# A selective scan in which GpSimd takes three of its sixteen output products, and its preparation runs a step earlier

## The chip, the cores and the metric

The kernel runs on one core of a Trainium2 chip. Its engines are TensorE (PE: matrix products and transposes into PSUM), VectorE (DVE), ScalarE (ACT), GpSimd (POOL) and SyncE (SP), which here only starts transfers. Each engine runs its own list of instructions in order, and semaphores hold an instruction back until another engine has done what it needs. The metric is the device time of one launch in microseconds (us). Before the change it was 1448.95 us, the median of three runs (1447.45 to 1464.47).

## The reference, cut to what matters

Two transformer-like layers run on 16 sequences of 256 positions with 128 features. Layer 0 has a decaying linear attention and a mixture of experts, layer 1 a selective scan (Mamba) and a second mixture of experts. The change touches the selective scan of layer 1 alone:

```python
proj = x @ W_in.T                       # x_s (256), z (256), B (16), C (16), dt (8)
x_s = silu(conv(x_s) + conv_b)          # depthwise, 4 taps
dt = softplus(dt @ W_dt.T + b_dt)
for t in range(256):                    # 256 channels d, 16 states n
    h[d, n] = exp(dt[t, d] * A[d, n]) * h[d, n] + dt[t, d] * B[t, n] * x_s[t, d]
    y[t, d] = sum_n h[d, n] * C[t, n]
y = (y + x_s * D) * silu(z)
out = layernorm(residual + y @ W_out.T)
```

## The kernel before, in words

`scan_phase` handles the 16 sequences one after another, b = 0 to 15. The 256 channels lie as two halves (h) on the 128 partitions, time along the free axis. A sequence is walked in eight **steps**, j = 0 to 7, of two states (n) each, so an operand of a step has 2 x 2 x 256 = 1024 elements in each partition. In a step

- ACT makes the decays `dA` (`decays`, four exponentials), three steps ahead, in a ring of four buffers;
- POOL multiplies the transposed input `dtuT` by four columns of B (`inputs`, line 1409, four instructions on 256 elements), also three steps ahead, in a ring of four (`dbuT`);
- PE copies the rows of C of this step to all partitions (`C_rows`, bank bC), transposes `dbuT` of the next step (`turn_inputs`, line 1532) and adds up the products of the step before (`sum_states`, line 1550);
- DVE runs the recurrence (`recur`, line 1181, one scan over 1024 elements into `hs`) and then the product with C (`times_C`, line 1189, 1024 elements into `hc`). `hs` and `hc` have two buffers each, used by even and odd steps.

Between these stands the work of the neighbouring sequences. `prepare(step, b + 1)` makes the next sequence's inputs: step 0 (normalized input `xn`, its transpose, and at 0.5 `hT`), 1 (projection of B, C and dt: `low`, `BT`, `bc`), 2 (ACT's six instructions of softplus, from `soft` = |x| to the last `soft`), 3 (convolution, PE), 4 (silu into `u` and `z`, between two loads of ACT's tables), 5 (`dtu` transposed into `dtuT`). `finish(step, b - 1)` ends the sequence before: 0 (DVE `yz`, PE transposes, ACT `yzT`), 1 (PE output projection), 2 (DVE statistics, ACT `olnv` and `orstd`), 3 (DVE `oshift`, ACT `oh`). POOL's shares are `split` and `keep` at j = 2, `cubic` at 3, `steps` (line 1369, dt) at 4, `times_u` (line 1383, `dtu`) and `residual` (lines 1389 to 1397) at 5. DVE's `lesser` (line 1154, `least`) is in step 4.

What sets the order is only how the code is written: each engine has a function `body` that walks j and issues its parts in turn. There is no scheduler. DVE's body is `recur`, then `finish`, then `lesser` if j is 4, then `times_C`; it waits in place wherever an input is late.

## Time and profile before

| | us |
|---|---|
| median of three runs | 1448.95 |
| the profiled execution, own time | 1469.19 |
| its span, first to last instruction | 1467.0 |
| DVE busy | 893.7 (61%) |
| PE busy | 1130.1 (77%) |
| ACT busy | 687.8 (47%) |
| POOL busy | 561.8 (38%) |
| scans of the 16 sequences (line 1181), first to last start | 514.6 to 999.9 |

The span counts from the first to the last instruction of one profiled execution. That execution took 1469.19 us, 20.24 us more than the median of the runs without a profile. The shares are averages over ten stages with different limits. The selective scan is one of them, about a third of the span. Busy time of PE is modelled, and overlaps between its instructions are counted once.

### The profile page before, as it was taken

The numbers are of one execution on the slowest core, as the hardware profiler recorded it, in microseconds if no ns is written. First come the engines' busy times: TensorE is split into PE (matmuls) and PEld (weight loads), VectorE is DVE, ScalarE is ACT, GpSimd is POOL, SyncE is SP. The second block draws the span as 40 slices with busy tenths as digits, with TensorE's granted clock in tenths as the row PEclk, the third lists the DMA queues.
The fourth block names the chain that finished last, engine by engine and source line by source line (L and its number), as shares of the span: only waits on it lengthen the run. The fifth ranks groups of instructions, "written<-read, shape, count | busy, mean of one in ns | idle before, by whom it ended". The sixth has DMA issues, their size and how long they took to land. (4 is left out here: it accounts for less than half of the span.)

```text
span 1467.0 us, 23954 instructions
## 1 busy us (share of the span) xinstructions
PE 1130.1 (77%) x6776; PEld 857.3 (58%) x6777; DVE 893.7 (61%) x1786; ACT 687.8 (47%) x1527; POOL 561.8 (38%) x882
## 2 busy tenths in 40 slices
PE   2887885689978688888888888883374799999860
PEld 1555554334448578777888877773243666666640
DVE  2355553711039599999999999993376633333327
ACT  1334432233324587888778887771241033333320
POOL 1000000300012277777877778770000155555540
PEclk9667775799989789999999999996555599999995
DMA  6000000011010200000000000002310011111115
GB/s 181 0 1 1 0 1 1 0 44 43 29 29 0 58 1 1 1 0 0 0 0 0 0 0 0 0 0 90 97 33 17 6 35 39 36 39 38 38 48 181
DMA packets 41607, 39.87 MB, mean 27 GB/s; under 512 B 4041, under 2 KB 37474, under 8 KB 41202
## 3 DMA queue, kind: packets, MB, share of 16 engines
q1 hardware_dynamic: 32466, 22.37, 5.2%
q0 software_dynamic: 4608, 9.45, 2.3%
q10 hardware_dynamic: 4496, 7.60, 1.5%
q8 instruction: 18, 0.29, 0.1%
q14 instruction: 19, 0.16, 0.0%
HBM read 30.44 MB, written 8.96 MB: 27 GB/s over the span
## 5 line engine op out<-in xcount | busy, mean ns | idle before, releaser
L1181 DVE TENSOR_TENSOR_SCAN s_hs<-s_dA,bank 128x1024 f32<-128x1024 f32 x128 | 291.9, 2280 | 10.2 <-PE bank L1532 10.1
L1409 POOL TENSOR_SCALAR s_dbuT<-s_dtuT,s_BT 128x256 f32<-128x256 f32 x512 | 239.9, 492 | 11.0 <-ACT s_dtuT L1264 8.8
L1292 ACT ACTIVATE s_dA<-s_dt,aneg 128x255 f32<-128x255 f32 x512 | 213.6, 498 | 0.6 <-DVE s_hs L1181 0.4
L1982 POOL DMA_INDIRECT x_xg<-hf_rows,x_src x72 | 69.7, 968 | 236.9 <-issue 170.6
L1532 PE MATMUL bank<-const,s_dbuT 128*128 128x128 f32 x1024 | 139.7, 282 | 26.0 <-POOL s_dbuT L1409 26.0
L1189 DVE TENSOR_TENSOR s_hc<-s_hs,bank 128x1024 f32<-128x1024 f32 x128 | 156.1, 1220 | 5.2 <-PE bank L1520 0.9
L2022 PE MATMUL bank<-w,x_xT 128*128 x288 | 128.4, 569 | 19.0 <-ACT x_xT L2064 16.3
L1550 PE MATMUL bank<-const,s_hc 128*128 128x128 f32 x1024 | 138.0, 280 | 2.2 <-DVE s_hc L1189 2.2
L1532 PEld LDWEIGHTS bank<-const,s_dbuT 128*128 128x128 f32 x1024 | 119.8, 145 | 32.7 <-issue 26.3
L1550 PEld LDWEIGHTS bank<-const,s_hc 128*128 128x128 f32 x1024 | 120.7, 145 | 2.4 <-DVE s_hc L1189 2.4
L2060 ACT ACTIVATE x_a<-bank 128x448 f32<-128x448 f32 x72 | 39.1, 543 | 161.6 <-PE bank L2022 156.7
L484 POOL COPY xn<-xb 128x512 f32 (+1 forms) x8 | 4.9, 612 | 213.3 <-ACT xb L500 213.3
L2022 PEld LDWEIGHTS bank<-w,x_xT 128*128 128x128 f32 x288 | 50.1, 194 | 56.5 <-issue 56.0
L1989 POOL DMA_INDIRECT y_rows<-x_y,x_dst x72 | 71.0, 987 | 29.3 <-issue 22.4
L2044 PE MATMUL bank<-w2d,x_hT 112*128 x576 | 77.8, 278 | 2.6 <-DVE x_y L2092 2.1
L965 POOL COPY yst<-yT 128x512 f32 (+1 forms) x16 | 16.1, 1031 | 166.1 <-POOLq L103 123.2
L920 DVE COPY yT<-bank 128x512 f32 x16 | 11.1, 692 | 110.5 <-PE bank L900 110.5
L2044 PEld LDWEIGHTS bank<-w2d,x_hT 112*128 112x128 f32 x576 | 69.9, 191 | 5.5 <-issue 4.4
L2080 DVE COPY x_src<-from_row 128x1 uint32 (+1 forms) x72 | 11.1, 154 | 100.8 <-PE bank L2031 96.0
L912 ACT ACTIVATE g<-bank 128x512 f32<-128x512 f32 x64 | 38.2, 597 | 58.7 <-PE bank L893 58.7
L893 PE MATMUL bank<-xin,w 128*128 x128 | 59.2, 618 | 5.9 <-DMA w<-in_w 5.9
L1520 PE MATMUL bank<-s_bc,spread 128*128 128x256 bf16 x256 | 50.7, 281 | 16.7 <-DVE s_hc L1189 14.7
(301 smaller groups left out, 2273.6 us busy)
## 6 DMA issues: line engine op xcount, KB each, us to landing
w<-in_w SPq DMA_DIRECT2D x16, 256.0 KB, 3.1
o_yr<-y_rows SPq DMA_DIRECT2D x8, 512.0 KB, 3.9
w<-in_w ACTq DMA_DIRECT2D x1, 3584.0 KB, 13.3
x_res<-in_x SPq DMA_DIRECT2D x4, 512.0 KB
gate<-gates_d SPq DMA_DIRECT2D x2, 1024.0 KB, 5.6
s_gate<-gates_d SPq DMA_DIRECT2D x2, 1024.0 KB, 7.4
hf_rows<-r_rows SPq DMA_DIRECT2D x8, 256.0 KB, 2.2
out<-o_o ACTq DMA_DIRECT2D x8, 256.0 KB, 2.4
```

The source lines that it names most:

```text
L893: pe.matmul(ps[h][:, :], w1[:, k, h * P:(h + 1) * P], m.xin[:, 2 * r + k, a * N:(a + 1) * N], start=True, stop=True).then_inc(hidden[h], 1)
L1181: dve.tensor_tensor_scan(flat(hs[:, j % 2]), flat(dA[:, j % RING]), bDbu[j % 2], 0.0, ALU.mult, ALU.add).then_inc(S["scanned"], 1)
L1189: dve.tensor_tensor(hc[:, j % 2], hs[:, j % 2], bC[:, :].rearrange("p (n t) -> p n t", n=2).unsqueeze(1).broadcast_to([P, NH, 2, L]), ALU. ...
L1292: ins = act.activation(dA[:, j % RING, h, n, 1:], dt[:, k, h, 1:], ACT.Exp, scale=m.aneg[:, h, 2 * j + n:2 * j + n + 1])
L1409: ins = pool.tensor_scalar(dbuT[:, j % RING, c, n, :], dtuT[:, k, c, :], BT[:, k, c, 2 * j + n:2 * j + n + 1], 1.0, ALU.mult, ALU.mult)
L1520: mm = pe.matmul(bC[:, n * L:(n + 1) * L], m.spread[:, 2 * j + n, :], bc[:, k, :], start=True, stop=True)
L1532: mm = pe.transpose(out[:, h, n, c * P:(c + 1) * P], dbuT[:, j % RING, c, n, h * P:(h + 1) * P], ident)
L1550: mm = pe.matmul(part(c, h), hc[:, j % 2, h, n, c * P:(c + 1) * P], ident, is_transpose=True, start=False, stop=(j == SCAN_J - 1 and n == ...
L1982: pool.indirect_dma_start(xg[k][:], None, m.hf_rows[:, :], bass.IndirectOffsetOnAxis(ap=src[k][:, 0:1], axis=0)).then_inc(S["rows"][k], 16)
L1989: pool.indirect_dma_start(m.y_rows[:, :], bass.IndirectOffsetOnAxis(ap=dst[k][:, 0:1], axis=0), y[k][:], None).then_inc(S["sent"][k], 16)
L2022: mm = pe.matmul(ps[2 * k + i][:, 0:I1], xT[:, k, :], m.w13[:, bass.ds(e * 2 + i, 1), :].rearrange("p e i -> p (e i)"), start=True, stop=True)
L2044: mm = pe.matmul(ps[5][:, 0:D], hT[:, k, i, :], m.w2d[:, bass.ds(e * NIC + i, 1), :].rearrange("p e d -> p (e d)"), start=(i == 0), stop=( ...
```

## The change

SHARED = (0, 5, 6) names three steps. In these DVE multiplies only the first of the two states by C (512 elements instead of 1024). The second is multiplied by a new function on POOL, `shared_C(b, j)`, which stands in POOL's step j + 1 behind `inputs`. It cannot read PSUM, so it takes its C row from SBUF: SP copies three rows of `low` to DRAM and from there to all 128 partitions (`Crow`), once per sequence. PE spreads one C row instead of two in these steps, and adds the shared product up two steps later (`sum_shared`). Two more waits are new on DVE: the scan of step j + 2 waits until POOL has read the buffer of step j (`shared`), and the product of step j + 2 until PE has read it (`y_shared`).

Beside this, parts of `prepare` move. PE does the projection still at j = 0, but ahead of step 1's recurrence work and behind `finish(0)`, and dt's product at j = 1 instead of 2; half of the convolution moves to j = 4; the skip product with D moves from `sum_states(0)` to `sum_states(1)`. ACT does softplus (prepare 2) at j = 1 instead of at the end of j = 2, and at j = 4 and 5 it does silu and the copy to `dtuT` ahead of the decays instead of behind them.

```diff
@@ -1060,2 +1060,3 @@
 AHEAD = 3
+SHARED = (0, 5, 6)
 
@@ -1070,2 +1071,3 @@
 
+
     with ExitStack() as ctx:
@@ -1099,2 +1101,4 @@
         hc = sb("hc", [P, 2, NH, 2, L])
+        Crow = sb("Crow", [P, 2, len(SHARED), L])
+        C_d = nc.dram_tensor("C_rows", (2, len(SHARED), L), F32).ap()
         yz = sb("yz", [P, NCH, DI])
@@ -1106,3 +1110,4 @@
                  "u_ready z_ready dt_ps pos abs ln soft dt_ready dtu_ready dtuT_ps dtuT hi r1 mid bc_parts oln gate "
-                 "yz yzT_ps yzT out_ps ostats ost ors oshift o_read og done").split()
+                 "yz yzT_ps yzT out_ps ostats ost ors oshift o_read og done "
+                 "C_kept C_spread shared y_shared").split()
         S = {n: sem(n) for n in names}
@@ -1180,2 +1185,6 @@
                 dve.wait_ge(S["dA_ready"], 8 * b + j + 1)
+                if j == 0:
+                    dve.wait_ge(S["shared"], len(SHARED) * b + 1)
+                elif j - 2 in SHARED:
+                    dve.wait_ge(S["shared"], len(SHARED) * b + SHARED.index(j - 2) + 2)
                 dve.tensor_tensor_scan(flat(hs[:, j % 2]), flat(dA[:, j % RING]), bDbu[j % 2], 0.0,
@@ -1188,5 +1197,10 @@
                     dve.wait_ge(S["y_part"], 8 * b + j - 1)
-                dve.tensor_tensor(hc[:, j % 2], hs[:, j % 2],
-                                  bC[:, :].rearrange("p (n t) -> p n t", n=2).unsqueeze(1).broadcast_to(
-                                      [P, NH, 2, L]), ALU.mult).then_inc(S["hc_ready"], 1)
+                if j == 0 and not first:
+                    dve.wait_ge(S["y_shared"], len(SHARED) * b)
+                elif j - 2 in SHARED:
+                    dve.wait_ge(S["y_shared"], len(SHARED) * b + SHARED.index(j - 2) + 1)
+                own = 1 if j in SHARED else 2
+                dve.tensor_tensor(hc[:, j % 2, :, 0:own], hs[:, j % 2, :, 0:own],
+                                  bC[:, 0:own * L].rearrange("p (n t) -> p n t", n=own).unsqueeze(1).broadcast_to(
+                                      [P, NH, own, L]), ALU.mult).then_inc(S["hc_ready"], 1)
 
@@ -1235,2 +1249,4 @@
                     act.wait_ge(S["bc_ps"], b + 1)
+                    if not (isinstance(b, int) and b == 0):
+                        act.wait_ge(S["C_kept"], 16 * len(SHARED) * b)
                     act.activation(low[:], bX[:, 0:L], ACT.Identity, bias=ident[:, 32 + RDT:33 + RDT])\
@@ -1297,2 +1313,4 @@
                 for j in range(SCAN_J):
+                    if prepares and j in (4, 5):
+                        prepare(j, b + 1, 1 - k)
                     if j + AHEAD < SCAN_J:
@@ -1301,10 +1319,10 @@
                         decays(b + 1, 1 - k, j + AHEAD - SCAN_J, True)
-                    if prepares and j != 2:
-                        prepare(j, b + 1, 1 - k)
-                    if not first:
-                        finish(j, b - 1, 1 - k)
                     if prepares and j == 0:
+                        prepare(0, b + 1, 1 - k)
                         prepare(0.5, b + 1, 1 - k)
-                    if prepares and j == 2:
-                        prepare(j, b + 1, 1 - k)
+                    if prepares and j == 1:
+                        prepare(1, b + 1, 1 - k)
+                        prepare(2, b + 1, 1 - k)
+                    if not first:
+                        finish(j, b - 1, 1 - k)
 
@@ -1332,2 +1350,22 @@
 
+            def spread_C(b, k):
+                sp.wait_ge(S["low"], b + 1)
+                if not (isinstance(b, int) and b == 0):
+                    sp.wait_ge(S["C_spread"], 16 * len(SHARED) * b)
+                for i, j in enumerate(SHARED):
+                    row = NST + 2 * j + 1
+                    sp.dma_start(C_d[k, i:i + 1, :], low[row:row + 1, :]).then_inc(S["C_kept"], 16)
+                sp.wait_ge(S["C_kept"], 16 * len(SHARED) * (b + 1))
+                if not (isinstance(b, int) and b <= 1):
+                    sp.wait_ge(S["shared"], len(SHARED) * (b - 1) + 1)
+                for i in range(len(SHARED)):
+                    sp.dma_start(Crow[:, k, i, :], C_d[k, i, :].partition_broadcast(P)).then_inc(S["C_spread"], 16)
+
+            spread_C(0, 0)
+            spread_C(1, 1)
+            with sp.Fori(0, PAIRS - 1, 1) as r:
+                spread_C(2 * r + 2, 0)
+                spread_C(2 * r + 3, 1)
+            sp.wait_ge(S["C_spread"], 16 * len(SHARED) * B)
+
         @block.gpsimd
@@ -1412,2 +1450,15 @@
 
+            def shared_C(b, k, j, first):
+                i = SHARED.index(j)
+                pool.wait_ge(S["C_spread"], 16 * len(SHARED) * (b + 1))
+                pool.wait_ge(S["scanned"], 8 * b + j + 1)
+                if j >= 2:
+                    pool.wait_ge(S["y_part"], 8 * b + j - 1)
+                elif not first:
+                    pool.wait_ge(S["y_part"], 8 * b + j - 1)
+                    pool.wait_ge(S["y_shared"], len(SHARED) * b)
+                pool.tensor_tensor(hc[:, j % 2, :, 1], hs[:, j % 2, :, 1],
+                                   Crow[:, k, i, :].unsqueeze(1).broadcast_to([P, NH, L]), ALU.mult)\
+                    .then_inc(S["shared"], 1)
+
             def body(b, k, first, prepares):
@@ -1422,2 +1473,4 @@
                         inputs(b + 1, 1 - k, j + AHEAD - SCAN_J, True)
+                    if j - 1 in SHARED:
+                        shared_C(b, k, j - 1, first)
                     if prepares and j == 2:
@@ -1433,2 +1486,3 @@
             pool.sem_inc(S["done"], 1)
+            pool.sem_inc(S["shared"], 1)
             pool.wait_ge(S["gate"], 32)
@@ -1469,6 +1523,6 @@
                     mm.then_inc(S["dt_ps"], 1)
-                if step == 3:
+                if step in (3, 3.5):
                     pe.wait_ge(S["abs"], b + 1)
                     pe.wait_ge(S["pos"], b + 1)
-                    for h in range(NH):
+                    for h in range(NH)[:1] if step == 3 else range(NH)[1:]:
                         for tap in range(KCONV):
@@ -1476,3 +1530,4 @@
                                            hT[:, k, tap:tap + L], start=(tap == 0), stop=(tap == KCONV - 1))
-                    mm.then_inc(S["xs_ps"], 1)
+                    if step == 3.5:
+                        mm.then_inc(S["xs_ps"], 1)
                 if step == 4:
@@ -1518,3 +1573,3 @@
                     pe.wait_ge(S["hc_ready"], 8 * b + j)
-                for n in range(2):
+                for n in range(1 if j in SHARED else 2):
                     mm = pe.matmul(bC[:, n * L:(n + 1) * L], m.spread[:, 2 * j + n, :], bc[:, k, :],
@@ -1537,6 +1592,6 @@
                 part = lambda c, h: bY[:, c * DI + h * P:c * DI + (h + 1) * P]
-                if j == 0:
+                if j == 0 and not first:
+                    pe.wait_ge(S["yz"], b)
+                if j == 1:
                     pe.wait_ge(S["u_ready"], 2 * b + 2)
-                    if not first:
-                        pe.wait_ge(S["yz"], b)
                     for c in range(NCH):
@@ -1544,5 +1599,5 @@
                             pe.matmul(part(c, h), u[:, k, h, c * P:(c + 1) * P], m.dskip[:, h, :],
-                                      start=(c == 0 and h == 0), stop=False, skip_group_check=True)
+                                      start=False, stop=False, skip_group_check=True)
                 pe.wait_ge(S["hc_ready"], 8 * b + j + 1)
-                for n in range(2):
+                for n in range(1 if j in SHARED else 2):
                     for c in range(NCH):
@@ -1550,3 +1605,3 @@
                             mm = pe.matmul(part(c, h), hc[:, j % 2, h, n, c * P:(c + 1) * P], ident,
-                                           is_transpose=True, start=False,
+                                           is_transpose=True, start=(j == 0 and n == 0 and c == 0 and h == 0),
                                            stop=(j == SCAN_J - 1 and n == 1), skip_group_check=True)
@@ -1554,2 +1609,10 @@
 
+            def sum_shared(b, j):
+                pe.wait_ge(S["shared"], len(SHARED) * b + SHARED.index(j) + 2)
+                for c in range(NCH):
+                    for h in range(NH):
+                        mm = pe.matmul(bY[:, c * DI + h * P:c * DI + (h + 1) * P], hc[:, j % 2, h, 1, c * P:(c + 1) * P],
+                                       ident, is_transpose=True, start=False, stop=False, skip_group_check=True)
+                mm.then_inc(S["y_shared"], 1)
+
             def body(b, k, first, prepares):
@@ -1557,2 +1620,6 @@
                     C_rows(b, k, j, first)
+                    if j - 2 in SHARED:
+                        sum_shared(b, j - 2)
+                    elif j == 0 and not first:
+                        sum_shared(b - 1, SCAN_J - 2)
                     if j + 1 < SCAN_J:
@@ -1565,8 +1632,12 @@
                         sum_states(b - 1, 1 - k, SCAN_J - 1, False)
-                    if prepares:
-                        prepare(j, b + 1, 1 - k)
+                    if prepares and j == 0:
+                        prepare(0, b + 1, 1 - k)
                     if not first:
                         finish(j, b - 1, 1 - k, prepares)
+                    if prepares:
+                        for step in {0: (1,), 1: (2,), 3: (3,), 4: (3.5, 4), 5: (5,)}.get(j, ()):
+                            prepare(step, b + 1, 1 - k)
 
             def last(b, k):
+                sum_shared(b, SCAN_J - 2)
                 sum_states(b, k, SCAN_J - 1, False)
@@ -1575,4 +1646,4 @@
 
-            for j in range(SCAN_J):
-                prepare(j, 0, 0)
+            for step in (0, 1, 2, 3, 3.5, 4, 5):
+                prepare(step, 0, 0)
             turn_inputs(0, 0, 0, True)
```

The first place is POOL from the end of `residual` on (`x_res<-x_res,s_og`), that is its steps 5 to 7 and the first two of the next sequence. Before:

```order
L1397 TENSOR_TENSOR x_res<-x_res,s_og 128x256
L1405 REGISTER_ALU
L1409 TENSOR_SCALAR s_dbuT<-s_dtuT,s_BT 128x256 x8
L1405 REGISTER_ALU
L1409 TENSOR_SCALAR s_dbuT<-s_dtuT,s_BT 128x256 x8
L1405 REGISTER_ALU
L1409 TENSOR_SCALAR s_dbuT<-s_dtuT,s_BT 128x256 x4
```

And with the change:

```order
L1435 TENSOR_TENSOR x_res<-x_res,s_og 128x256
L1443 REGISTER_ALU
L1447 TENSOR_SCALAR s_dbuT<-s_dtuT,s_BT 128x256 x8
L1454 REGISTER_ALU
L1460 TENSOR_TENSOR s_hc<-s_hs,s_Crow 128x2x256
L1443 REGISTER_ALU
L1447 TENSOR_SCALAR s_dbuT<-s_dtuT,s_BT 128x256 x4
L1454 REGISTER_ALU
L1456 REGISTER_ALU
L1460 TENSOR_TENSOR s_hc<-s_hs,s_Crow 128x2x256
```

The product of step 5 now stands behind `residual` and behind the eight `dbuT` instructions of the next sequence's steps 0 and 1; the product of step 6 follows four more.

The second place is ACT in the steps 1 and 2, from the projection's outputs to `orstd`, the scale of the layer norm of the sequence before. Before:

```order
L1236 ACTIVATE s_low<-bank,const 128x256
L1238 ACTIVATE s_BT<-bank 128x32
L1240 ACTIVATE s_bc<-bank 128x256
L1289 REGISTER_ALU
L1292 ACTIVATE s_dA<-s_dt,aneg 128x255 x4
L1273 ISA
L1274 ACTIVATE s_olnv<-s_omv,eps 128x2
L1276 ACTIVATE s_orstd<-s_olnv 128x2
L1244 ACTIVATE s_soft<-bank 128x512
```

And with the change:

```order
L1256 ACTIVATE s_bc<-bank 128x256
L1260 ACTIVATE s_soft<-bank 128x512
L1261 ACTIVATE s_pos<-bank 128x512
L1263 ACTIVATE s_e<-s_soft 128x512
L1265 ACTIVATE s_sq<-s_e,eps 128x512
L1266 ACTIVATE s_over<-s_e,eps 128x512
L1268 ACTIVATE s_soft<-s_over,eps 128x512
L1305 REGISTER_ALU
L1308 ACTIVATE s_dA<-s_dt,aneg 128x255 x4
L1289 ISA
L1290 ACTIVATE s_olnv<-s_omv,eps 128x2
L1292 ACTIVATE s_orstd<-s_olnv 128x2
```

The six softplus instructions, which stood behind `orstd`, now stand ahead of it and of the decays of step 5.

## Rows read from the trace of the kernel before

**Rows 1.** Busy time by engine in a stretch of the scan stage.
```profile
core 0: us, PE busy (x) PEld busy (x) DVE busy (x) ACT busy (x) POOL busy (x), PEclk, DMA share, GB/s
800.00:900.00 100.00, 88.81 (x666) 79.59 (x665) 95.87 (x80) 80.46 (x179) 76.92 (x141) 0.98 0.00 0
```

**Rows 2.** Single lines: duration in ns (min/median/max), first and last start.
```profile
L1181 DVE TENSOR_TENSOR_SCAN s_hs<-s_dA,bank x128: 2278/2280/2289, 514.6 to 999.9; 128x1024 f32<-128x1024 f32 x128
...
L1189 DVE TENSOR_TENSOR s_hc<-s_hs,bank x128: 1210/1221/1223, 516.9 to 1002.2; 128x1024 f32<-128x1024 f32 x128
```

**Rows 3.** Timeline, DVE (start, us, line, operation): scans that open sequences 1 and 15.
```profile
544.21 2.28 DVE L1181 TENSOR_TENSOR_SCAN s_hs<-s_dA,bank 128x1024 f32<-128x1024 f32 x1
...
974.10 2.28 DVE L1181 TENSOR_TENSOR_SCAN s_hs<-s_dA,bank 128x1024 f32<-128x1024 f32 x1
```

**Rows 4.** Timeline, DVE: step 2 of one sequence to step 1 of the next.
```profile
829.61 2.28 DVE L1181 TENSOR_TENSOR_SCAN s_hs<-s_dA,bank 128x1024 f32<-128x1024 f32 x1
...
833.73 2.28 DVE L1181 TENSOR_TENSOR_SCAN s_hs<-s_dA,bank 128x1024 f32<-128x1024 f32 x1
835.92 0.13 DVE L1174 SCALAR_TENSOR_TENSOR s_oshift<-s_omv,s_orstd 128x2 f32<-128x2 f32 x1
...
837.18 2.28 DVE L1181 TENSOR_TENSOR_SCAN s_hs<-s_dA,bank 128x1024 f32<-128x1024 f32 x1
839.37 0.88 DVE L1154 TENSOR_TENSOR s_least<-s_small,s_soft 128x512 f32<-128x512 f32 x1
...
841.54 2.28 DVE L1181 TENSOR_TENSOR_SCAN s_hs<-s_dA,bank 128x1024 f32<-128x1024 f32 x1
...
851.90 2.28 DVE L1181 TENSOR_TENSOR_SCAN s_hs<-s_dA,bank 128x1024 f32<-128x1024 f32 x1
854.54 0.69 DVE L1160 TENSOR_TENSOR s_yz<-bank,s_z 128x512 f32<-128x512 f32 x1 [0.36 <-PE bank L1550]
856.28 2.28 DVE L1181 TENSOR_TENSOR_SCAN s_hs<-s_dA,bank 128x1024 f32<-128x1024 f32 x1
```

**Rows 5.** Timeline, POOL, the same sequence, steps 5 to 7.
```profile
844.42 1.27 POOL L1383 TENSOR_TENSOR s_dtu<-s_dt,s_u 128x512 f32<-128x512 f32 x1 [1.68 <-ACT s_u L1256]
...
848.61 10.91 POOL L1409 TENSOR_SCALAR s_dbuT<-s_dtuT,s_BT 128x256 f32<-128x256 f32 x24 [0.30 <-ACT s_dtuT L1264]
```

**Rows 6.** Timeline, ACT, the same sequence, steps 2 to 6.
```profile
832.71 0.29 ACT L1274 ACTIVATE s_olnv<-s_omv,eps 128x2 f32<-128x2 f32 x1
...
834.60 0.60 ACT L1244 ACTIVATE s_soft<-bank 128x512 f32<-128x512 f32 x1 [1.37 <-PE bank L1467]
...
838.23 1.69 ACT L1292 ACTIVATE s_dA<-s_dt,aneg 128x255 f32<-128x255 f32 x4
...
843.51 0.84 ACT L1256 ACTIVATE s_u<-bank,bcol 128x256 f32<-128x256 f32 x2
...
847.75 0.57 ACT L1264 ACTIVATE s_dtuT<-bank 128x512 f32<-128x512 f32 x1
```

**Rows 7.** Timeline, PE, step 7 and the next sequence's steps 0 to 3.
```profile
850.58 1.09 PE L1532 MATMUL bank<-const,s_dbuT 128*128 128x128 f32 x8 [1.60 <-POOL s_dbuT L1409]
...
855.29 0.66 PE L1500 MATMUL bank<-const,s_yz 128*128 128x128 f32 x4 [0.57 <-DVE s_yz L1160]
...
859.29 0.60 PE L1457 MATMUL bank<-s_hT,w_in 128*128 128x256 f32 x2
...
863.57 1.13 PE L1467 MATMUL bank<-s_low,wdt 9*128 9x256 f32 x4
...
866.60 3.62 PE L1475 MATMUL bank<-s_hT,wc 128*128 128x256 f32 x16
```

**Rows 8.** Where PE's granted clock was 0.50: busy times, and DVE's timeline beside them.
```profile
820.00:822.00 2.00, 2.00 (x11) 2.00 (x11) 1.52 (x2) 2.00 (x6) 2.00 (x6) 0.50 0.00 0
...
820.66 2.29 DVE L1181 TENSOR_TENSOR_SCAN s_hs<-s_dA,bank 128x1024 f32<-128x1024 f32 x1 [0.48 <-PE bank L1532]
...
824.42 0.69 DVE L1160 TENSOR_TENSOR s_yz<-bank,s_z 128x512 f32<-128x512 f32 x1 [1.47 <-PE bank L1550]
```

More of the change, by code:

```diff
@@ L1565, in body @@
                         sum_states(b - 1, 1 - k, SCAN_J - 1, False)
-                    if prepares:
-                        prepare(j, b + 1, 1 - k)
+                    if prepares and j == 0:
+                        prepare(0, b + 1, 1 - k)
                     if not first:
                         finish(j, b - 1, 1 - k, prepares)
+                    if prepares:
+                        for step in {0: (1,), 1: (2,), 3: (3,), 4: (3.5, 4), 5: (5,)}.get(j, ()):
+                            prepare(step, b + 1, 1 - k)
             def last(b, k):
+                sum_shared(b, SCAN_J - 2)
                 sum_states(b, k, SCAN_J - 1, False)
```

3 lines of the change are left out of this document (1 added, 2 removed).

## The prediction

> **What bounds the kernel now.** I read the busy times by stretch first. In the scan stage DVE is busy for 95.87 of 100 us, PE for 88.81, ACT for 80.46 and POOL for 76.92 [rows 1]. So DVE sets the pace here, and nothing outside this stage is touched. The first and the last start of the scans, 514.6 and 999.9 us, bound what the change can reach [rows 2]. From the opening scan of sequence 1 to that of sequence 15 there are 14 sequences in 429.89 us, 30.71 us each [rows 3].
>
> Next comes DVE's timeline through one undisturbed sequence. I write T0 to T7 for the starts of its eight scans. A plain step takes 3.45 us: T5 to the next T0 is 10.36 us for three [rows 4]. Step 2 takes 4.12 us because of the statistics, step 4 4.36 us because of `least`, step 0 4.38 us because of `yz`, of which 0.36 us is a wait for PE [rows 4]. The sum is 4.38 + 3.45 + 4.12 + 3.45 + 4.36 + 10.36 = 30.12 us. The mean is 0.6 us above it, and rows 8 show why: in some sequences PE's granted clock is 0.50 (1.2 GHz instead of 2.4 GHz) around the turn to the next sequence, and `yz` starts 3.76 us behind its scan (824.42 against 820.66) instead of 2.64 us (854.54 against 851.90) [rows 4, 8]. Ahead of it PE stood still for 1.60 us, waiting for POOL's `dbuT` [rows 7].
>
> **What the change gives.** A product with C over 1024 elements takes 1.22 us [rows 2]. The nearest row of half that size with one operand in PSUM is `yz`, 0.69 us [rows 4]. So each of the three shared steps gives DVE 0.53 us, a step of 2.92 us instead of 3.45, and a sequence 1.6 us, if nothing waits. PE spreads three C rows fewer; this I cost at nothing, since PE then only waits longer for DVE.
>
> **What it adds on POOL.** Three products of 128x512, like `dtu`'s 1.27 us [rows 5]. Both operands and the output are in SBUF there too, so I take 1.27 for each, between 0.69 (DVE's time for the size, below which POOL will not come) and 2 us. The Trainium skill advises against such a move (GPSIMD Engine Reference, section 4.1, Engine selection: elementwise work with two inputs belongs on VectorE, about twice as slow on GpSimd). Twice 0.69 would be 1.38, an estimate from that page, and would add 0.1 us to a sequence; the trace's ratio is 1.84, so it agrees.
>
> More than its length, the product's place counts. The product of step 5 stands in POOL's list behind `dtu`, the three instructions of `residual` and eight `dbuT` of the next sequence, as the first pair of order listings shows. DVE's scan of step 7 now waits for it, since it overwrites the same `hs` buffer, and behind that scan everything on DVE is queued. I follow this chain from T4.
>
> 1. PE begins its part of step 4 at T4 + 0.15 (the product of step 3 is then done). From the dt product to the convolution is 3.03 us (863.57 to 866.60), of which the dt product itself is 1.0; so C rows, transposes and sum take 2.0 [rows 7]. The half of the convolution that is now in step 4 takes half of 3.62 us [rows 7]. It is done by T4 + 4.1, and ACT begins `u` at T4 + 4.2.
> 2. From `u` to the start of the `dtuT` copy ACT needs 4.24 us (843.51 to 847.75): `u`, `z`, a table load and four decays. The new order has the same instructions between them. The copy takes 0.57 [rows 6]: done at T4 + 9.0.
> 3. POOL begins `dtu` 0.91 us after `u` (844.42 against 843.51), at T4 + 5.1, and the `dbuT` 4.19 us after that (848.61), `residual` being between [rows 5, 6]: T4 + 9.3. Moving silu up has brought this point forward: before, it was T4 + 11.43 (848.61 against 837.18) [rows 4, 5].
> 4. 24 `dbuT` take 10.91 us, 0.455 each [rows 5]. Eight take 3.64, then the product 1.27: T4 + 14.2. DVE starts scan 7 at T4 + 14.3.
>
> DVE by itself would be there at 4.36 + 2.92 + 2.92 = T4 + 10.2. **So it waits 4.1 us in each sequence.** The next T0 comes 3.45 later, T4 + 17.75; the product of step 6 (four more `dbuT` and 1.27, to T4 + 17.3) is just in time.
>
> **The second new wait.** Softplus now stands ahead of the decays of step 5 and of `orstd` on ACT (second pair of order listings), but DVE still takes `oshift` in step 3, and behind it stands the product that ends the step. From T0: `yz` starts at 2.7 (four transposes more, but PE comes earlier), and step 0 takes 2.7 + 1.74 - 0.53 = 3.9 [rows 4]. PE begins the `yzT` transposes 0.75 later, and the projection 0.42 after that, at 3.9. From the projection to the dt product is 4.28 us (859.29 to 863.57), less 0.44 for half a group of transposes: 7.7 [rows 7]. The dt product takes 1.13, so `soft` starts at 8.9 [rows 7]. From `soft` to the decays are 3.63 us (834.60 to 838.23), the decays keep ACT 1.6, `olnv` and `orstd` 0.5 [rows 6]: 14.65. DVE would start `oshift` 2.19 behind T3 [rows 4], and T3 is 3.9 + 3.45 + 4.12 = 11.5, so at 13.7. It waits 1.0 us, and T4 is at 11.5 + 3.45 + 1.05 = 16.0.
>
> **The sum.** A sequence takes 14.3 + 3.45 + 16.0 = 33.75 us at full clock. PE now idles some 3.8 us ahead of the product of step 5, where 1.60 us of idling preceded the low clock in about one sequence of three. When the clock is low there, everything from `yz` on is 1.1 us later (3.76 - 2.64) [rows 4, 8]. I take that for three sequences in four: 0.85, together 34.6. The Trainium skill (TensorE: Matmul & The Clock Gate, What's actually happening) says that the clock is held back by default and activity releases it; by this every sequence would pay, 4 us more in all.
>
> Against 30.71 this is 3.9 more in each of 14 sequences, 54.6 us. Sequence 0 has no `finish` and pays about 2 us, sequence 15 prepares nothing, so POOL is free and 1.6 us are gained; these cancel. The profiled execution would go from 1469.19 to 1524 us. The median lies 20.24 us under the profiled time, and both shift alike: 1448.95 + 55 = **1504 us**, 3.8% slower.
>
> The two copies of C between SBUF and DRAM are costed at nothing: `low` is ready in step 1, and POOL needs the rows in the next sequence's step 0, over 20 us later. If this cover failed, POOL would wait for them in front of everything of step 1.
>
> **The rivals.**
>
> - *Only the wait of step 7 is real* (0.2). ACT reaches `orstd` in time, because PE's chain from `yz` to the dt product is shorter than added up here; the margin is only 1.0 us. Then 34.6 - 1.05 = 33.55, 14 x 2.84 = 40: 1489 us; with the clock low as seldom as before, 1482.
> - *DVE stays the bound* (0.08, the other side). Point of decision: POOL ends the product of step 5 by T4 + 10.2. Then the steps are 30.12 - 1.6 = 28.5, 14 x 2.2 + 3.2 = 34 us less: 1415 us, 2.3% faster. For it speaks that silu moves up and DVE is at 96%. Against it: `dbuT` would have to start by T4 + 5.3, but `least` alone ends at T4 + 3.07 (839.37 + 0.88 against 837.18) [rows 4], and after it come `dt` and `dtu` of about 1.27 each and `residual`.
> - *The waits nearly cancel the gain* (0.14): `residual` or the copy to `dtuT` costs POOL less than in the old order, and the chain is 2 to 3 us shorter. Then the time is 1430 to 1475 us.
> - *Both waits, and PE falls behind as well* (0.1): low clock in all sequences and for longer, 1 us more each: 1518 to 1535 us.
> - *Both waits as added up* (0.48): 1490 to 1518 us.
>
> That the change doesn't do what it says is hardly possible: the order shows the three products and the halved operands.
>
> The range is 1466 to 1520 us; it leaves out the faster case, the lower part of the near-cancelling one and the upper part of the last. About 2% is what a measurement of this kernel can tell from no change; within it lie 1420 to 1478 us. Faster by over 2%: 0.06; within 2%: 0.16; slower: 0.78.
>
> **What would show it.** The line of DVE's scan has idle time of some 55 us before it, released by POOL's `hc`, all of it at step 7; with none there the forecast falls. `oshift` has some 14 us of idle before it, released by ACT's `orstd`. The halved products take 0.69 us and POOL's 1.27. From one opening scan to the next are 34 to 35 us. PE waits for the same POOL product just ahead. If the step 7 scan starts within 11 us of T4, the chain through `dtu` and `residual` was wrong.

## The result and the profile after

The changed kernel takes 1509.51 us (median of 4 runs, 1504.30 to 1512.35). The kernel before took 1450.03 us beside it (4 runs, 1447.45 to 1464.47). The ratio is 1.036, 95% interval 1.032 to 1.041: **slower**. The ratio is estimated with its interval and isn't exactly the quotient of the medians; by it the loss is 53 us, by the medians 59.5, and 55 were forecast.

The profiled execution took 1509.2 us. First the page's span and busy times:

```profile
span 1507.4 us, 24350 instructions
PE 1137.1 (75%) x6728; PEld 865.8 (57%) x6729; DVE 869.2 (58%) x1786; ACT 689.5 (46%) x1527; POOL 615.4 (41%) x930
```

The span grew by 40.4 us only, but this understates the loss: in the profile of before, the opening scan starts at 514.6 us [rows 2], here at 503.3, and the change gives no engine other work ahead of it. From the opening scan to the last one are 485.3 us before and 539.8 now (503.32 to 1043.11), **54.5 us more**. This is the number that the sum of the prediction has to meet. It lies between the two estimates of the loss; runs of the kernel before differ by 17 us among themselves, so I assign no more than this.

The groups of instructions in the scan stage (line, engine, operation, operands, count | busy us, mean ns | idle time just before them in us, and what ended it):

```profile
L1190 DVE TENSOR_TENSOR_SCAN s_hs<-s_dA,bank 128x1024 f32<-128x1024 f32 x128 | 291.8, 2280 | 75.7 <-POOL s_hc L1460 66.5 <-PE bank L1587 9.1
L1203 DVE TENSOR_TENSOR s_hc<-s_hs,bank 128x1024 f32<-128x1024 f32 x80 | 97.3, 1216 | 4.8 <-PE bank L1614 2.1 <-PE bank L1575 1.6
L1203 DVE TENSOR_TENSOR s_hc<-s_hs,bank 128x512 f32<-128x512 f32 x48 | 32.9, 684 | 1.6 <-PE bank L1575 0.5
L1460 POOL TENSOR_TENSOR s_hc<-s_hs,s_Crow 128x512 f32<-128x512 f32 x48 | 61.0, 1272 | 5.3 <-DVE s_hs L1190 3.6 <-issue 1.6
L1179 DVE SCALAR_TENSOR_TENSOR s_oshift<-s_omv,s_orstd 128x2 f32<-128x2 f32 x16 | 4.9, 306 | 11.9 <-ACT s_orstd L1292 11.9
```

The halved product takes 684 ns on DVE and the other half 1272 ns on POOL, so each of the 48 shared products saves DVE 0.53 us of work, as costed: 25 us in all. Ahead of the scans, however, DVE now stands idle for 66.5 us, waiting for POOL's `hc`, and 11.9 us ahead of `oshift`. The saving was real, and the waits were three times as large.

The waits of steady sequences, 560 to 1020 us (total us, times, longest):

```profile
DVE s_hs L1190 <- POOL s_hc L1460: 61.1, 14, 4.4
PE bank L1614 <- POOL s_hc L1460: 55.2, 14, 4.0
...
DVE s_oshift L1179 <- ACT s_orstd L1292: 10.5, 13, 0.8
```

There is one wait of 4.4 us in a sequence, and one of 0.8. The timelines of ACT, DVE, POOL and PE show where, in a sequence whose T4 is 863.79:

```profile
862.17 0.20 ACT L1292 ACTIVATE s_orstd<-s_olnv 128x2 f32<-128x2 f32 x1
862.41 0.33 DVE L1179 SCALAR_TENSOR_TENSOR s_oshift<-s_omv,s_orstd 128x2 f32<-128x2 f32 x1 [0.80 <-ACT s_orstd L1292]
863.79 2.27 DVE L1190 TENSOR_TENSOR_SCAN s_hs<-s_dA,bank 128x1024 f32<-128x1024 f32 x1
...
867.83 0.84 ACT L1272 ACTIVATE s_u<-bank,bcol 128x256 f32<-128x256 f32 x2 [1.87 <-PE bank L1529]
868.75 1.28 POOL L1421 TENSOR_TENSOR s_dtu<-s_dt,s_u 128x512 f32<-128x512 f32 x1 [0.74 <-ACT s_u L1272]
...
872.22 0.57 ACT L1280 ACTIVATE s_dtuT<-bank 128x512 f32<-128x512 f32 x1
873.07 3.65 POOL L1447 TENSOR_SCALAR s_dbuT<-s_dtuT,s_BT 128x256 f32<-128x256 f32 x8 [0.44 <-ACT s_dtuT L1280]
876.68 1.27 POOL L1460 TENSOR_TENSOR s_hc<-s_hs,s_Crow 128x512 f32<-128x512 f32 x1
877.98 2.29 DVE L1190 TENSOR_TENSOR_SCAN s_hs<-s_dA,bank 128x1024 f32<-128x1024 f32 x1 [4.36 <-POOL s_hc L1460]
878.00 1.11 PE L1614 MATMUL bank<-const,s_hc 128*128 128x128 f32 x4 [3.94 <-POOL s_hc L1460]
```

Read it from the last scan backwards: it starts 0.03 us behind the end of POOL's product; that product starts when the eight `dbuT` ahead of it end; these start when ACT's `dtuT` copy has ended. PE waits for the same product. No wait of POOL names the copies of C through DRAM that the change adds.

### The profile page after: what moved, and what is told of

Read it like the earlier page. It is cut to its first block and busy times, and to the rows that moved or that the text cites. A ratio compares the mean times of both kernels' runs of the same rounds, so it can differ in the third digit from the quotient of the medians.

```text
span 1507.4 us, 24350 instructions
## 1 busy us (share of the span) xinstructions
PE 1137.1 (75%) x6728; PEld 865.8 (57%) x6729; DVE 869.2 (58%) x1786; ACT 689.5 (46%) x1527; POOL 615.4 (41%) x930
## 5 line engine op out<-in xcount | busy, mean ns | idle before, releaser
L1190 DVE TENSOR_TENSOR_SCAN s_hs<-s_dA,bank 128x1024 f32<-128x1024 f32 x128 | 291.8, 2280 | 75.7 <-POOL s_hc L1460 66.5
L1447 POOL TENSOR_SCALAR s_dbuT<-s_dtuT,s_BT 128x256 f32<-128x256 f32 x512 | 234.5, 479 | 14.0 <-ACT s_dtuT L1280 10.8
L1587 PE MATMUL bank<-const,s_dbuT 128*128 128x128 f32 x1024 | 149.8, 295 | 2.8 <-POOL s_dbuT L1447 2.8
L1587 PEld LDWEIGHTS bank<-const,s_dbuT 128*128 128x128 f32 x1024 | 130.9, 155 | 7.2 <-POOL s_dbuT L1447 3.0
L1203 DVE TENSOR_TENSOR s_hc<-s_hs,bank 128x1024 f32<-128x1024 f32 (+1 forms) x128 | 130.2, 1017 | 6.5 <-PE bank L1575 2.1
L1605 PE MATMUL bank<-const,s_hc 128*128 128x128 f32 x832 | 119.2, 284 | 1.7 <-DVE s_hc L1203 1.7
L1605 PEld LDWEIGHTS bank<-const,s_hc 128*128 128x128 f32 x832 | 101.3, 147 | 2.0 <-DVE s_hc L1203 2.0
L1614 PE MATMUL bank<-const,s_hc 128*128 128x128 f32 x192 | 42.9, 366 | 60.0 <-POOL s_hc L1460 60.0
L1614 PEld LDWEIGHTS bank<-const,s_hc 128*128 128x128 f32 x192 | 30.7, 190 | 64.7 <-POOL s_hc L1460 64.2
L1575 PE MATMUL bank<-s_bc,spread 128*128 128x256 bf16 x208 | 46.3, 286 | 27.1 <-DVE s_hc L1203 27.1
```

The source lines that it names most:

```text
L1190: dve.tensor_tensor_scan(flat(hs[:, j % 2]), flat(dA[:, j % RING]), bDbu[j % 2], 0.0, ALU.mult, ALU.add).then_inc(S["scanned"], 1)
L1203: dve.tensor_tensor(hc[:, j % 2, :, 0:own], hs[:, j % 2, :, 0:own], bC[:, 0:own * L].rearrange("p (n t) -> p n t", n=own).unsqueeze(1).bro ...
L1447: ins = pool.tensor_scalar(dbuT[:, j % RING, c, n, :], dtuT[:, k, c, :], BT[:, k, c, 2 * j + n:2 * j + n + 1], 1.0, ALU.mult, ALU.mult)
L1575: mm = pe.matmul(bC[:, n * L:(n + 1) * L], m.spread[:, 2 * j + n, :], bc[:, k, :], start=True, stop=True)
L1587: mm = pe.transpose(out[:, h, n, c * P:(c + 1) * P], dbuT[:, j % RING, c, n, h * P:(h + 1) * P], ident)
L1605: mm = pe.matmul(part(c, h), hc[:, j % 2, h, n, c * P:(c + 1) * P], ident, is_transpose=True, start=(j == 0 and n == 0 and c == 0 and h == 0),
```

## The experiments

us per sequence are the distances between opening scans in a steady stretch of the profiled execution. The kernels were measured in three groups (the first four rows, the next four, the last three), each on another chip and beside runs of its own of the kernel before (medians 1457.07, 1452.13 and 1436.31 us), so they are compared by their ratios to it (estimated as above, not quotients of the medians). "After" stands for the changed kernel, 34.1 us per sequence, and before has 30.71.

| kernel | median us | ratio to before, 95% interval | us per sequence |
|---|---|---|---|
| moves alone | 1453.41 | 0.998 (0.995 to 1.001) | 30.4 |
| sharing alone | 1522.66 | 1.044 (1.037 to 1.051) | 34.7 to 35.9 |
| after, shared product first | 1484.74 | 1.016 (1.008 to 1.024) | 31.7 to 32.0, four of 33.8 to 34.1 |
| after, orstd early | 1508.54 | 1.031 (1.024 to 1.039) | 34.1 |
| after, PE kept busy | 1503.97 | 1.038 (1.030 to 1.046) | 33.7 |
| after, POOL reordered | 1455.12 | 1.003 (0.999 to 1.006) | 30.55 |
| both of these orders | 1444.60 | 0.994 (0.990 to 0.998) | 29.6 |
| both, two shared | 1438.64 | 0.993 (0.990 to 0.996) | 29.2 |
| the same, again | 1416.45 | 0.988 (0.985 to 0.990) | 29.2, two of 30.85 |
| moves and orstd early | 1421.01 | 0.990 (0.988 to 0.993) | 29.5 |
| both, one shared | 1413.95 | 0.985 (0.983 to 0.987) | 29.2 |

The theory at the outset was that of the prediction: scan 7 waits for POOL's product of step 5 because of its place in POOL's list. The first rivals were that the moved preparation costs the time, and that it is the extra work on POOL, wherever it stands.

### Each part of the change alone

The kernel of moves alone has ACT's and PE's order of the changed kernel, but all products whole on DVE, with no rows of C through DRAM. Against after:

```diff
-                own = 1 if j in SHARED else 2
-                dve.tensor_tensor(hc[:, j % 2, :, 0:own], hs[:, j % 2, :, 0:own],
+                dve.tensor_tensor(hc[:, j % 2], hs[:, j % 2],
...
-                    if j - 1 in SHARED:
-                        shared_C(b, k, j - 1, first)
```

> The kernel before with the moved preparation and the moved skip product alone; DVE makes all sixteen products. Theory (the loss is the wait of scan 7 for POOL's product of step 5, plus the wait of oshift): the 4.4 us wait at step 7 is gone, the dbuT instructions come earlier and PE's idle time ahead of them shrinks with the low clock, but oshift still waits for orstd, 0.5 to 1 us, and the first sequence is some 4 us longer. About the time before, 1445 to 1460 us. Rival (the moves themselves cost the time): 1490 us or more.

Measured: 0.998 of before, 30.4 us per sequence, and no idle time at all ahead of the scans. It keeps the new wait at `oshift`. Two groups of the stretch 560 to 960 us:

```profile
L1181 DVE TENSOR_TENSOR_SCAN s_hs<-s_dA,bank 128x1024 f32<-128x1024 f32 x106 | 241.5, 2278 | 0.0
L1174 DVE SCALAR_TENSOR_TENSOR s_oshift<-s_omv,s_orstd 128x2 f32<-128x2 f32 x13 | 4.7, 361 | 10.2 <-ACT s_orstd L1276 10.2
```

So the moves cost nothing in sum, and the whole loss hangs on the sharing, or on the sharing with them. They carry a loss of their own, though: 0.78 us a sequence ahead of `oshift`, which itself takes 0.36 us instead of 0.13, so that step 3 takes 1.0 us more. Something else gave this back (step 4 is 3.91 us instead of 4.36, and the extra time of step 0 at low clock is gone).

Sharing alone is after with the ACT and PE order of before (the skip product with D keeps its new place):

```diff
-                    if prepares and j in (4, 5):
-                        prepare(j, b + 1, 1 - k)
...
+                    if prepares:
+                        prepare(j, b + 1, 1 - k)
...
-                        for step in {0: (1,), 1: (2,), 3: (3,), 4: (3.5, 4), 5: (5,)}.get(j, ()):
-                            prepare(step, b + 1, 1 - k)
```

> The shared products without the moved preparation (projection, softplus, convolution, silu stand where they stood before). Theory: the dbuT instructions start 11.4 us behind T4 as before instead of 9.3, so scan 7 waits about 2 us longer, 6.3 us, while the wait of oshift is gone: 34.9 us per sequence, 1510 to 1522 us. Rival (the moves cost more than they give): below 1495 us.

Measured: 1.044, 1522.66 us, just above the 1510 to 1522 us expected. The two starts of `dtu` and `dbuT` and the scan of step 7 in its timeline (scan 5 is at 902.89):

```profile
905.78 1.26 POOL L1419 TENSOR_TENSOR s_dtu<-s_dt,s_u 128x512 f32<-128x512 f32 x1 [1.69 <-ACT s_u L1272]
...
909.98 3.65 POOL L1445 TENSOR_SCALAR s_dbuT<-s_dtuT,s_BT 128x256 f32<-128x256 f32 x8 [0.34 <-ACT s_dtuT L1280]
...
914.89 2.29 DVE L1190 TENSOR_TENSOR_SCAN s_hs<-s_dA,bank 128x1024 f32<-128x1024 f32 x1 [6.08 <-POOL s_hc L1458]
```

`dtu` starts 2.9 us behind scan 5; in after it is 1.05 (868.75, with scan 5 3.91 behind T4). The wait is 6.1 instead of 4.4 us (6.3 were expected). So the moves shorten the very wait that the sharing makes, as step 3 of the prediction said.

### The product's place in POOL's list

In each step of POOL, the shared product goes ahead of the four or eight `dbuT` instead of behind them:

```diff
+                    if j - 1 in SHARED:
+                        shared_C(b, k, j - 1, first)
                     if j + AHEAD < SCAN_J:
                         inputs(b, k, j + AHEAD, not (first and j + AHEAD < RING))
                     elif prepares:
                         inputs(b + 1, 1 - k, j + AHEAD - SCAN_J, True)
-                    if j - 1 in SHARED:
-                        shared_C(b, k, j - 1, first)
```

> The changed kernel with one thing else: in each step of POOL the shared product stands ahead of the four dbuT instead of behind them. Theory (place in POOL's list): the product of step 5 ends four dbuT earlier, 1.82 us, so the wait of scan 7 falls from 4.36 to about 2.5 us and 14 times 1.8 = 25 us are gained: 1484 us. Rival (POOL's total work or a slow product is the limit): no gain, 1509 us.

Measured: 1.016, and the wait of step 7 falls by 1.8 us, the time of four `dbuT`. The waits of 560 to 1020 us and one place in the timelines of DVE and POOL:

```profile
DVE s_hs L1190 <- POOL s_hc L1460: 35.8, 14, 2.6
```
```profile
657.13 1.84 POOL L1447 TENSOR_SCALAR s_dbuT<-s_dtuT,s_BT 128x256 f32<-128x256 f32 x4 [0.45 <-ACT s_dtuT L1280]
658.93 1.27 POOL L1460 TENSOR_TENSOR s_hc<-s_hs,s_Crow 128x512 f32<-128x512 f32 x1
660.23 2.29 DVE L1190 TENSOR_TENSOR_SCAN s_hs<-s_dA,bank 128x1024 f32<-128x1024 f32 x1 [2.56 <-POOL s_hc L1460]
```

POOL does the same work in both kernels. This settles that the place, and not the amount of work, sets the length of the wait. In four sequences step 0 took 5.85 to 6.12 us instead of 3.9 to 4.1: there the granted clock was at 0.50 from 2 to 3 us ahead of the opening scan to more than 4 us behind it, over `yz`, and took some 2 us. In seven others it fell to 0.50 too, but was back at the latest 0.7 us behind the opening scan, and `yz` started 2.66 to 2.93 us behind that scan, as in the sequences at full clock (2.66 to 2.81).

Then the product of step 5 right behind `dtu`, with `residual` moved a step earlier, so that it waits for no `dbuT` at all (step 0's stays where it is):

```diff
-                    if not first and j == 5:
-                        residual(b - 1)
+                    if j == 5 and 5 in SHARED:
+                        shared_C(b, k, 5, first)
...
-                    if j - 1 in SHARED:
-                        shared_C(b, k, j - 1, first)
+                    if j == 1 and 0 in SHARED:
+                        shared_C(b, k, 0, first)
+                    if j == 6 and 6 in SHARED:
+                        shared_C(b, k, 6, first)
...
+                    if not first and j == 4:
+                        residual(b - 1)
```

> The changed kernel with POOL's list in another order and the same work: residual stands in step 4 ahead of dt, where POOL idles 3.1 us; the product of step 5 directly behind dtu; the product of step 6 behind the dbuT of step 1 of the next sequence. Theory (the loss is the place of the product of step 5): scan 7 no longer waits for POOL, 4.4 us less per sequence, then POOL with 29 us of work per sequence is the next bound: 30 to 30.7 us per sequence, 1448 to 1462 us. Rival (the product slows DVE or is itself the limit wherever it stands): above 1485 us.

Measured: 1.003, 30.55 us per sequence; step 6 takes 2.92 us, and the wait ahead of scan 7 is gone. POOL and DVE in its timeline:

```profile
705.28 1.27 POOL L1401 TENSOR_TENSOR s_small<-s_cub,s_e 128x512 f32<-128x512 f32 x1
...
712.64 1.27 POOL L1421 TENSOR_TENSOR s_dtu<-s_dt,s_u 128x512 f32<-128x512 f32 x1 [0.18 <-ACT s_u L1272]
714.05 1.28 POOL L1460 TENSOR_TENSOR s_hc<-s_hs,s_Crow 128x512 f32<-128x512 f32 x1
...
716.90 3.67 POOL L1447 TENSOR_SCALAR s_dbuT<-s_dtuT,s_BT 128x256 f32<-128x256 f32 x8 [1.57 <-ACT s_dtuT L1280]
720.54 1.27 POOL L1460 TENSOR_TENSOR s_hc<-s_hs,s_Crow 128x512 f32<-128x512 f32 x1
```
```profile
705.69 0.87 DVE L1179 SCALAR_TENSOR_TENSOR s_oshift<-s_omv,s_orstd 128x2 f32<-128x2 f32 x1 [0.81 <-ACT s_orstd L1292]
...
721.84 2.29 DVE L1190 TENSOR_TENSOR_SCAN s_hs<-s_dA,bank 128x1024 f32<-128x1024 f32 x1 [0.78 <-POOL s_hc L1460]
```

The wait is gone at scan 7, but the same chain through ACT's `dtuT` and the eight `dbuT` now holds the product of step 6, and with it the next opening scan, for 0.78 us. So the time came out as expected, but the next bound is this chain and not POOL's amount of work: POOL is busy 267 of 300 us, and idles 1.57 us ahead of the eight `dbuT`. Against the kernel of moves alone, steps 0, 5 and 6 give 1.5 us, while step 7 (+0.86), step 3 (+0.55, `oshift` takes 0.87 us itself) and step 4 (+0.17) take 1.6. That is why three shared products without the big wait are no faster than none.

### The wait of oshift

ACT takes `olnv` and `orstd` ahead of the decays of the step:

```diff
+                    if not first and j == 2:
+                        finish(2, b - 1, 1 - k)
                     if j + AHEAD < SCAN_J:
                         decays(b, k, j + AHEAD, not (first and j + AHEAD < RING))
...
-                    if not first:
+                    if not first and j != 2:
```

> The changed kernel with olnv and orstd ahead of the decays of step 5 on ACT. Theory: orstd is ready 1.6 us earlier, the 0.80 us wait of oshift vanishes with its consequence of about 0.2 us, 14 x 1.0 = 14 us: 1495 us, the step 7 wait unchanged at 4.4 us. Rival (the wait of oshift is covered by the longer one of scan 7): no change, 1509 us.

Measured: 1.031, 34.1 us per sequence as in after: **the expectation missed**. The 0.80 us ahead of `oshift` did go (step 3 takes 3.46 us instead of 4.47), but step 6 takes 7.98 instead of 7.37 and step 0 mostly 4.7 to 4.8 instead of 4.37. Timelines of PE, DVE and ACT, and the busy times of one stretch (the number behind those of the five engines is PE's granted clock):

```profile
860.53 1.90 PE L1531 MATMUL bank<-s_hT,wc 128*128 128x256 f32 x8
861.50 2.28 DVE L1190 TENSOR_TENSOR_SCAN s_hs<-s_dA,bank 128x1024 f32<-128x1024 f32 x1
...
866.16 0.84 ACT L1272 ACTIVATE s_u<-bank,bcol 128x256 f32<-128x256 f32 x2 [1.47 <-PE bank L1531]
...
876.31 2.29 DVE L1190 TENSOR_TENSOR_SCAN s_hs<-s_dA,bank 128x1024 f32<-128x1024 f32 x1 [4.98 <-POOL s_hc L1462]
...
883.31 0.69 DVE L1165 TENSOR_TENSOR s_yz<-bank,s_z 128x512 f32<-128x512 f32 x1 [1.26 <-PE bank L1607]
```
```profile
880.00:882.00 2.00, 2.00 (x12) 2.00 (x12) 2.00 (x1) 1.11 (x3) 2.00 (x5) 0.55 0.00 0
```

T4 (861.50) comes a microsecond earlier, but PE is then still at the first half of the convolution, so `u` starts at T4 + 4.66 instead of T4 + 4.04, and the chain behind it ends 0.6 us later with respect to T4. In this order PE, not DVE, starts that chain. The rest went into step 0: `yz` waits 1.26 us for PE instead of 0.86. With it goes a low clock that comes later: PE stands still for 4.55 us instead of 3.94 ahead of the product of step 5, and the granted clock is back 2.0 us behind the opening scan (879.77) instead of 1.2 us behind it. That this accounts for the 0.4 us was not tried by itself; the next section shows what the low clock costs in after.

With the order of POOL that has the product of step 5 right behind `dtu`, and the same ACT edit:

> The order of the run before in this call and olnv and orstd ahead of the decays of step 5. Theory: the 0.8 us wait of oshift goes too; DVE alone would need 29.3 us per sequence, POOL about 29: 29.5 to 30 us, 1433 to 1448 us. Rival (POOL saturated): as the run before, no gain from orstd.

Measured: 0.994, 29.6 us per sequence instead of 30.55. Here, where nothing holds scan 7, the same edit is worth its whole microsecond, as expected.

### The low clock at the turn

PE gets nine products of 256 columns whose results nobody reads, in step 7, to stay busy in the gap:

```diff
+                    if prepares and j == 7:
+                        pe.wait_ge(S["dtuT"], b + 2)
+                        for i in range(9):
+                            pe.matmul(bX[:, 0:L], m.wc[:, 0, 0:P], hT[:, k, 0:L], start=True, stop=True)
```

> The changed kernel with nine matmuls of 256 columns more on PE in step 7, between the C rows and the transposes that wait for POOL's product of step 5; their result is not used. They fill PE's idle time there. Theory (the low clock behind that idle time delays yz and with it the turn of the sequence): the granted clock stays high in that stretch, step 0 goes from 4.37 to 3.9 us and the sequence from 34.12 to some 33.6: 1502 us. The waits for POOL stay. Rival (the clock costs nothing, the wait for POOL absorbs it): no change, 1509 us, or slower if the added work makes PE late.

Measured: 1.038; by its interval not told apart from after (1.036). Its profile is clearer than its times: a granted clock of 1.00 over 300 us, and 33.6 to 33.8 us per sequence instead of 34.1, all of it in step 0 (3.86 to 3.98 instead of mostly 4.3 to 4.4). This is the step and the size that were expected. Busy times, first of this kernel, then of after around one scan 7:

```profile
600.00:900.00 300.00, 268.02 (x1960) 238.38 (x1959) 246.75 (x206) 221.06 (x489) 239.75 (x410) 1.00 0.04 12
```
```profile
874.00:876.00 2.00, 0.07 (x1) 0.00 (x0) 0.00 (x0) 2.00 (x6) 2.00 (x5) 0.95 0.00 0
876.00:878.00 2.00, 0.00 (x0) 0.00 (x0) 0.02 (x1) 1.56 (x4) 2.00 (x4) 0.50 0.00 0
878.00:880.00 2.00, 2.00 (x10) 2.00 (x11) 2.00 (x1) 0.00 (x0) 2.00 (x5) 0.50 0.00 0
880.00:882.00 2.00, 2.00 (x11) 1.69 (x10) 1.97 (x3) 1.70 (x5) 2.00 (x4) 0.50 0.00 0
882.00:884.00 2.00, 2.00 (x17) 2.00 (x16) 1.72 (x1) 0.78 (x3) 2.00 (x5) 0.84 0.00 0
```

In after, PE stands still for 3.9 us, the clock falls to 0.50 (1.2 GHz) at each of the 15 turns and is back before the next `yz`. By the periods (34.12 against 33.71 us) this costs 0.4 us per sequence.

### How much sharing pays

Both orders, and products shared in steps 0 and 5 only:

```diff
-SHARED = (0, 5, 6)
+SHARED = (0, 5)
```

> As the kernel before in this call, but only steps 0 and 5 are shared; DVE makes the whole product of step 6. DVE needs 0.53 us more per sequence, POOL 1.27 us less. Theory: if POOL is the bound of the three-step version, this is faster than it by up to 0.7 us per sequence (10 us); if DVE is, slower by 7 us.

Measured: 0.993 against 0.994 with three shared, so their intervals overlap; the period is 0.37 us shorter, between the two values expected. Run again on another chip:

> The same kernel as two_shared, to stand beside these two on one chip: 29.2 us per sequence, 0.993 of the kernel before.

Measured: 0.988. One kernel's ratio moved by 0.5% between the two groups, and the intervals only touch, at 0.990. A difference of this size between kernels of different groups therefore says nothing. Its steady period is 29.2 us both times, with two sequences of 30.85 in the second. DVE is then nearly full, 289.5 of 300 us:

```profile
600.00:900.00 300.00, 270.53 (x2077) 243.27 (x2076) 289.46 (x237) 252.80 (x563) 265.45 (x460) 1.00 0.03 9
```

Nothing shared, but the moves and the early `orstd` (the edits of the first and the fourth kernel of the table together):

> No product shared at all: the moved preparation of moves_only, and olnv and orstd ahead of the decays of step 5. Theory (the sharing itself gives something once nothing waits): 30.43 less 1.03 us of oshift's wait is 29.4 us per sequence, 1437 to 1443 us, behind the version with two shared steps (29.2 us). Rival (most of what two_shared gained came from the order, not from the sharing): level with it within 0.5%.

Measured: 0.990, 29.5 us per sequence. In the same group two shared products gave 0.988, and the intervals (0.988 to 0.993, and 0.985 to 0.990) overlap: level within 0.5%, as the rival had it. And one product shared, that of step 5 (`SHARED = (5,)`):

> As two_shared, with step 5 alone shared. The shared product of step 0 ends behind the time at which scan 2 could start (step 2 takes 4.51 us instead of 4.12), so leaving it out costs DVE 0.53 us and spares the wait and 1.27 us of POOL: 28.9 to 29.2 us per sequence, level with two_shared or up to 4 us faster. Rival (DVE's work alone counts): 0.5 us more per sequence, 7 us slower.

Measured: **0.985, the lowest ratio of all**, 1413.95 us beside 1436.31 for the kernel before, with the 29.2 us per sequence that were expected. Its list of waits in steady sequences has no wait of DVE among its largest:

```profile
ACT s_soft L1260 <- PE bank L1527: 35.4, 13, 2.7
POOL s_og L1429 <- ACT s_oh L1297: 22.3, 13, 1.7
POOL s_dbuT L1449 <- PE bank L1593: 10.1, 15, 0.7
```

The two intervals (0.983 to 0.987, and 0.988 to 0.993 with nothing shared) lie apart, in one group. So sharing one product, with POOL's new order, is worth 0.5% by the ratios; the scans of the 16 sequences take 464.6 us, first to last start, against 469.7. `residual`'s earlier place was not tried alone. In the steps the gain stands at step 5, which takes 2.91 us instead of 3.45, and step 3 takes back some 0.2. Two thirds of the gain over before come from the moves with `orstd` early, and need no sharing. One and two shared products are not told apart (0.983 to 0.987 against 0.985 to 0.990, same group).

## Why the prediction was right

The steps by their numbers in the prediction, for the sequence shown above; they rest on one timeline, but every sequence from 2 to 14 takes 34.08 to 34.18 us.

| step | forecast | measured |
|---|---|---|
| 1: `u` starts | T4 + 4.2 | T4 + 4.04 |
| 2: `dtuT` copy ends | T4 + 9.0 | T4 + 9.0 |
| 3: `dbuT` starts | T4 + 9.3 | T4 + 9.28 |
| 4: scan 7 starts | T4 + 14.3 | T4 + 14.19 |
| wait of scan 7 | 4.1 us | 4.36 us |
| wait of `oshift` | 1.0 us | 0.80 us, and 0.33 instead of 0.13 for itself |
| step 0 without the low clock | 3.9 | 3.9 (with PE kept busy) |
| low clock, per sequence | 1.1 us in three of four, 0.85 on average | 0.4 us in all |
| sequence, opening scan to opening scan | 34.6 | 34.1 |
| sequence 0 | +2 | +7.6 |
| sequence at full clock | 33.75 | 33.7 (with PE kept busy) |
| sequence 15 | -1.6 | -0.65 |

**The mechanism held.** The place of the product in POOL's list sets scan 7. Against the 4.4 us of wait in after, edits of that place or of what stands ahead of it moved the wait with the length of the chain: 6.1 us with the old order of ACT and PE, 5.0 with `u` 0.6 us later, 2.6 with four `dbuT` fewer ahead, none with `dtu` ahead alone. The wait is 4.36 us where 4.1 were forecast, because scan 7 starts as forecast but DVE would be there sooner: step 4 takes 3.91 us instead of 4.36, with `least` at 0.66 us instead of 0.88 and no idle time behind it. The rival that DVE stays the bound fell with the same rows; it needed the product's end at T4 + 10.2, and that is 877.95, T4 + 14.16. The rival that the wait of step 7 alone is real fell by `oshift`'s 0.80 us. Its reasoning would have been off even with `orstd` in time: removing that wait alone gave nothing in after, not the 1.05 us per sequence that I set for it.

**Two sizes were off, and they cancel in part.** The low clock was priced from `yz` 3.76 against 2.64 us behind its scan [rows 4, 8], where it lay over the product of the turn. In after the idling of PE ends 6.6 us ahead of `yz` (878.00 and 884.59), so most of the low stretch lies where PE catches up anyway. The low clock came more often than the three in four that I took, and cost under half of the 1.1. Nor does the 1.60 us of idling explain how often it came before: in the trace of before PE waits 1.60 us ahead of each turn from sequence 2 on, and the clock is low at five of them. On how often, the rule cited in the prediction (the Trainium skill, TensorE: Matmul & The Clock Gate, What's actually happening) had it right: the granted clock fell in each sequence. Its 4 us in all would have been added on the wrong price.

Sequence 0 was sized by eye, "about 2 us", and that term failed. It took 37.15 us, where before it took 29.59. Steps 1 and 2 take 4.2 us more, steps 4 to 6 take 3.9 more, and step 0 gives 0.5. This is DVE's timeline, then PE's:

```profile
510.13 1.22 DVE L1203 TENSOR_TENSOR s_hc<-s_hs,bank 128x1024 f32<-128x1024 f32 x1 [1.60 <-PE bank L1575]
...
537.01 2.29 DVE L1190 TENSOR_TENSOR_SCAN s_hs<-s_dA,bank 128x1024 f32<-128x1024 f32 x1 [5.34 <-POOL s_hc L1460]
```
```profile
506.37 0.69 PE L1506 MATMUL bank<-const,s_xn 128*128 128x128 f32 x2 [1.16 <-ACT s_xn L1240]
507.71 1.22 PE L1511 MATMUL bank<-s_hT,w_in 128*128 128x256 f32 x2 [0.66 <-ACT s_hT L1246]
```

The next sequence's projection now stands on PE ahead of the C rows of step 1, waits for ACT, and holds DVE's product: steps 1 and 2 take 5.5 and 5.9 us instead of 3.45 and 3.8. In the kernel of moves alone the same steps take 5.0 and 4.6, so 2.4 of these 4.2 us belong to the moves; the rest came with the sharing. The wait of scan 7 is 5.34 us instead of 4.36. Here too PE is late: it begins the C rows of step 4 1.8 us behind T4 (522.91 against 521.12) where in the steady sequence it is 0.13 us, `u` starts at T4 + 5.7 instead of T4 + 4.04, and scan 7 at T4 + 15.9 instead of T4 + 14.2.

Sequence 15 still finishes a sequence, and gave 0.65 us, which is step 5 and 6 (0.54 each) less 0.44 that step 2 lost. Step 0 gave nothing there: it is 4.37 us at the low clock, and 3.92 with PE kept busy. Why step 2 lost time was not looked into.

**The sum, measured.** 14 sequences of 34.11 against 30.71 us give 47.6 us (54.6 forecast); sequence 0 gives 7.6, sequence 15 takes 0.65: 54.5 us, which is the stage's growth. The 14 sequences came out 7 us under the forecast, 6 of them by the price of the clock (0.85 against 0.4 us each); sequences 0 and 15, which were to cancel, came to 6.9. That the total of 55 us was met to half a microsecond is luck. The verdict and the range do not rest on it: with either size put right alone, the forecast would have been 1498 or 1511 us.

## What to carry to other kernels

Work given to a second engine is priced by what stands ahead of it in that engine's list at the moment its result is due, not by its length: 1.27 us of work cost 4.4 us of wait behind eight instructions that had nothing to do with it, and nothing at scan 7 when it stood right behind `dtu`. Taking away one of two waits of a loop gives its length only where no other engine starts the chain that ends in the other wait; check that before you count it (`oshift`: 0 us in one order, 1 us in the other). And the first trip of a pipelined loop has waits of its own, so it needs its own chain in the sum. Before work is shared at all, the order is worth trying by itself: here it gave two thirds of the best gain.
